# A recommender tower on one core: the first group's products by selection matmuls, layer 0 in three-matmul form, and work moved between GpSimd, ScalarE and VectorE

## The reference

```python
# e: (512, 32 fields, 32);  filter_0: (32*32, 128);  filter_1: (32*128, 128)
z   = einsum('bhd,bmd->bhmd', e, e).reshape(b, 32*32, d)
c   = relu(einsum('bpd,pn->bnd', z, filter_0))
z1  = einsum('bhd,bmd->bhmd', e, c).reshape(b, 32*128, d)
c1  = relu(einsum('bpd,pn->bnd', z1, filter_1))
h   = concat([c.sum(-1), c1.sum(-1), dense_ctx], axis=1)
y   = relu(relu(h @ W_top1 + b_top1) @ W_top2 + b_top2) @ W_top3
```

## Time and profile before

| | us |
|---|---|
| median of 3 runs | 870.16 (868.09 to 870.87) |
| profiled execution, whole | 867.69 |
| its span, first to last instruction | 865.9 |
| TensorE busy, share of the span | 842.2 (97%) |
| ScalarE | 798.3 (92%) |
| GpSimd | 754.7 (87%) |
| VectorE | 747.8 (86%) |

### The profile page before, as it was taken

The page is one execution under the profiler, slowest core; times in us unless marked ns, Lnnn a source line. Parts: engine busy times, 40 slices in busy tenths (PEclk is TensorE's granted clock), DMA queues, the critical chain, the costliest instruction groups (busy, mean ns, idle before and its releaser), DMA issues.

```text
span 865.9 us, 16597 instructions
## 1 busy us (share of the span) xinstructions
PE 842.2 (97%) x3584; PEld 667.0 (77%) x3584; DVE 747.8 (86%) x800; ACT 798.3 (92%) x2781; POOL 754.7 (87%) x544
## 2 busy tenths in 40 slices
PE   2899999999999999999999999999999999999998
PEld 1688777778877777887777887777788777788776
DVE  4588888998888898888889888889888888988894
ACT  2699999999999999999999999999999999999994
POOL 5599999999999999999999999999999899997661
PEclk9999999999999999999999999999999999999999
DMA  5452222212222211222221222222122222122000
GB/s 163 140 148 83 77 81 83 60 34 78 80 77 81 80 47 44 82 76 80 82 79 28 64 82 76 80 81 54 36 81 79 77 81 69 35 69 73 2 1 1
DMA packets 42924, 61.11 MB, mean 71 GB/s; under 512 B 6259, under 2 KB 17139, under 8 KB 42902
## 3 DMA queue, kind: packets, MB, share of 16 engines
q1 hardware_dynamic: 38806, 58.75, 22.2%
q0 software_dynamic: 4096, 2.11, 1.6%
HBM read 56.64 MB, written 4.20 MB: 70 GB/s over the span
## 4 chain that ended last, share of the span: by engine, by line
PE 94%; DVE 2%; DMA 2%; issue 1%; SPq 0%; POOL 0%; ACT 0%; DVEq 0%; POOLq 0%
PE ps_y L685 27%; PE ps_y L686 27%; PE ps_y L691 27%; PE ps_c L664 6%; PE ps_c L674 2%; PE ps_c L672 2%; PE ps_c L673 2%; DVE csum L581 1%; PE ps_c L670 1%; DMA second<-et_scratch 1%; DVE prod L568 1%; DMA gat<-table,rows_now 1%; PE ps_h L696 0%; POOL gat L306 0%; DMA et_scratch<-gat 0%
## 5 line engine op out<-in xcount | busy, mean ns | idle before, releaser
L433 ACT ACTIVATE prod<-ps_y,es 128x128 f32<-128x128 f32 x2560 | 720.8, 456 | 26.8 <-PE ps_y L691 21.0
L581 DVE TENSOR_REDUCE csum<-prod 128x64 f32<-128x1536 f32 x256 | 446.4, 1744 | 0.1
L685 PE MATMUL ps_y<-w_hi,c_hi 128*128 128x512 f32 x1024 | 428.5, 419 | 0.9 <-ACT c_hi L394 0.5
L691 PE MATMUL ps_y<-w_hi,c_lo 128*128 128x512 f32 x1024 | 400.2, 391 | 0.0
L686 PE MATMUL ps_y<-w_lo,c_hi 128*128 128x512 f32 x1024 | 400.1, 391 | 0.0
L568 DVE TENSOR_TENSOR prod<-ps_y,es 128x512 f32<-128x512 f32 x384 | 259.0, 681 | 89.9 <-PE ps_y L691 89.8
L344 POOL TENSOR_TENSOR prod<-prod 128x1024 f32<-128x1024 f32 x128 | 309.1, 2415 | 27.4 <-ACT prod L433 22.0
L685 PEld LDWEIGHTS ps_y<-w_hi,c_hi 128*128 128x128 f32 x1024 | 192.5, 188 | 56.3 <-issue 10.5
L686 PEld LDWEIGHTS ps_y<-w_lo,c_hi 128*128 128x128 f32 x1024 | 192.5, 188 | 53.7 <-issue 14.9
L691 PEld LDWEIGHTS ps_y<-w_hi,c_lo 128*128 128x128 f32 x1024 | 192.2, 188 | 42.1
L335 POOL TENSOR_TENSOR z<-first,second 128x512 f32<-128x512 f32 x155 | 198.7, 1304 | 9.7 <-DMA second<-et_scratch 9.7
(11 more groups left out here) (96 smaller groups left out, 287.2 us busy)
## 6 DMA issues: line engine op xcount, KB each, us to landing
second<-et_scratch SPq DMA_DIRECT2D x160, 256.0 KB, 4.3
first<-et_scratch SPq DMA_DIRECT2D x32, 256.0 KB, 3.3
et_scratch<-gat SPq DMA_DIRECT2D x64, 64.0 KB
prod<-w SPq DMA_DIRECT2D x4, 512.0 KB, 7.8
gat<-table,rows_now POOLq DMA_INDIRECT x128, 2.4
wt_sb<-wt SPq DMA_DIRECT2D x2, 512.0 KB
prod<-w0a SPq DMA_DIRECT2D x1, 320.0 KB, 3.3
prod<-w0b SPq DMA_DIRECT2D x1, 320.0 KB, 3.3
```

Of the source, the lines that this page charges most:

```text
L433: last = nc.scalar.activation(prod[:, buffer_of(g, u), h // 2, :, h % 2], ps_y[:, bank_of(g, u, k), j * N:(j + 1) * N], ACT.Copy, scale=es ...
L581: nc.vector.tensor_reduce(csum[:, g.r, maps, u], prod[:, buffer_of(g, u), FOLD // 2:F // 2, maps, :].rearrange("p a n t -> p n a t"), AX.X ...
L685: nc.tensor.matmul(out, hi, w_hi, start=True, stop=False)
L691: nc.tensor.matmul(out, lo, w_hi, start=False, stop=True).then_inc(y_ready, 1)
```

## The change

1. **Head.** Group 0 no longer goes through the HBM scratch. A table `picks` of zeros and ones is loaded (its place zeroed first by POOL), and PE multiplies the gathered rows by it: 6 loads of 4 fp32 matmuls with 128 columns put `first` and the five `second` into PSUM banks. ACT copies `first` out, DVE multiplies (chunk 4 first). Chunks 0 to 3 of group 0 stay fp32. `filter_1`'s first quarter is loaded ahead of `filter_0`, the others after the first gather; its rounding is spread over the head and group 0. The warm-up is 10 matmuls and no longer waits for the gather. The first three groups' gathers read their indices without a staging copy.
2. **Layer 0** from group 1 on: `WHOLE = 0`, so chunks 0 and 1 are split too: two more `z_hi` on ACT, two more `z_lo` on POOL, three fp32r matmuls each in place of one fp32 matmul.
3. **`h0`** is summed by DVE from `c_hi` and `c_lo` side by side (1024 columns in place of 512), and ACT's `rectify_whole` goes.
4. **Parts** are rectified by POOL, behind its fold of `u = 1`.
5. **Fold.** `FOLD = 6`: POOL adds 3 field pairs to 3 (768 columns in place of 1024), DVE sums 13 pairs in place of 12.
6. **Staging** of the indices is a DMA that SP issues one group early.

The diff, cut to its core:

```diff
-WHOLE = 2
+WHOLE = 0
-WARM_UP = 22
+WARM_UP = 10
+FIRST_ROWS = SLOTS * TG
+PICKS = {"first": 0, 0: 1, 1: 2, 2: 3, 3: 4, 4: 5}
+PICK_ORDER = (4, 0, 1, 2, 3)
-FOLD = F // 4
+FOLD = 6
...
+        picks_sb = sb("picks_sb", [P, BT, 2, P + P // 2])
+        c_both = sb("c_both", [P, SLOTS, 2 * COLS], F32R)
...
             sp.dma_start(bounds_sb[:, :], bounds).then_inc(ids_in, 16)
+            filters(0)
             sp.dma_start(w0a_sb, w0a).then_inc(w0_in, 16)
             sp.dma_start(w0b_sb, w0b).then_inc(w0_in, 16)
             sp.dma_start(copy_sb[:, :], copy_of).then_inc(w0_in, 16)
+            sp.wait_ge(picks_zeroed, 1)
+            for q in range(BT):
+                sp.dma_start(picks_sb[q * F:(q + 1) * F, q, :, :], picks).then_inc(picks_in, 16)
             sp.dma_start(ones_b[:, :], ones_of_b).then_inc(ones_in, 16)
+            sp.wait_ge(gathered[0], 16 * TG)
+            for n in range(1, W1_LOADS):
+                filters(n)
+            def stage(g):
+                sp.dma_start(rows_now[:, g.r, :], rows[:, bass.ds(g.times(TG), TG)]).then_inc(rows_staged, 16)
+            def pairs(g, following=False):
                 cols = g.times(COLS)
                 sp.wait_ge(gathered[g.r], g.uses(16 * TG))
                 sp.sem_inc(sp_passed, 1)
+                if following:
+                    stage(g.plus(1))
...
-            pairs(Group(0, 0))
             for g in range(1, SLOTS):
                 pairs(Group(0, g))
...
                 if 0 in tiles:
-                    stage(g)
+                    pool.wait_ge(es_ready, g.times(1, 1 - SLOTS))
+                    wait(pool, et_written, g.times(32, -32 * SLOTS))
+                    pool.wait_ge(rows_staged, g.times(16, 16 * (1 - SLOTS)))
+                    pool.sem_inc(pool_passed, 1)
...
+            def rectify_parts(g):
+                pool.wait_ge(reduced, g.times(TG * HALVES, TG * HALVES))
+                wait(pool, c1_ready, g.times(1))
+                pool.sem_inc(pool_passed, 1)
+                nc.gpsimd.tensor_scalar(c1_parts[:, :, :], csum[:, g.r, :, :], 0.0, None, ALU.max).then_inc(parts_rectified, 1)
...
+            nc.gpsimd.memset(picks_sb[:, :, :, :], 0.0).then_inc(picks_zeroed, 1)
             pool.wait_ge(rows_step, 5)
-            for g in range(SLOTS):
-                gather(Group(0, g), range(TG))
+            for n in range(FIRST_ROWS):
+                pool.indirect_dma_start(
+                    out=gat[:, n // TG, n % TG * D:(n % TG + 1) * D], out_offset=None, in_=table,
+                    in_offset=bass.IndirectOffsetOnAxis(ap=rows[:, n:n + 1], axis=0),
+                ).then_inc(gathered[n // TG], 16)
-            Z_AT = {0: ((1, 1), (1, 2), (1, 3)), 1: ((1, 4),), 3: ((2, 0),)}
-            Z_LO_AT = {1: (2, 3), 2: (4,)}
+            Z_AT_FIRST = {0: ((1, 0), (1, 1), (1, 2)), 1: ((1, 3), (1, 4)), 3: ((2, 0), (2, 1))}
+            Z_LO_AT_FIRST = {1: (0, 1), 2: (2, 3, 4)}
+            Z_AT = {0: ((1, 2), (1, 3)), 1: ((1, 4),), 3: ((2, 0), (2, 1))}
+            Z_LO_AT = {0: (0, 1), 1: (2, 3), 2: (4,)}
...
                     fold(g, u)
+                    if u == 1 and number != 0:
+                        rectify_parts(g.plus(-1))
...
+            round_w1((0, 1))
+            act.wait_ge(picked, 1)
+            nc.scalar.activation(first[:, :], ps_y[:, PICKS["first"], :], ACT.Copy).then_inc(first_copied, 1)
+            act.wait_ge(w0_in, 48)
+            act.wait_ge(z_ready, 1)
+            nc.scalar.activation(z_hi[:, LASTK, :], z[:, LASTK, :], ACT.Copy, scale=copy_sb[:, 0:1]).then_inc(z_hi_ready, SPLIT)
+            round_w1((2, 3, 4, 5))
+            rectify_first(slice(0, 1), first_c_hi)
+            rectify_first(slice(1, TG), c_hi_ready)
+            round_w1((6, 7))
...
-                        if (u, k) == (1, 6) and number != 0:
-                            rectify_parts(g.plus(-1))
-                        if more and (u, k) == (3, 6):
-                            rectify_whole(g.plus(1))
-            Z_HI_AT = {(1, 2): (0, 4), (1, 3): (0, 6), (1, 4): (1, 5)}
+            Z_HI_AT = {(2, 0): (3, 4), (2, 1): (3, 7), (1, 2): (0, 2), (1, 3): (0, 5), (1, 4): (1, 5)}
...
+            def multiply_picked(k, place):
+                dve.wait_ge(picked, place)
+                nc.vector.tensor_tensor(z[:, k, :], first[:, :], ps_y[:, PICKS[k], :], ALU.mult).then_inc(z_ready, 1)
...
-                dve.wait_ge(c_ready, g.times(1, 1))
+                dve.wait_ge(c_lo_ready, g.times(1, 1))
                 nc.vector.tensor_reduce(
-                    h0[:, bass.ds(g.times(GB), GB)], c[:, :].rearrange("p (o b d) -> p b o d", b=GB, d=DT),
+                    h0[:, bass.ds(g.times(GB), GB)],
+                    c_both[:, g.r, :].bitcast(F32).rearrange("p (o b d) -> p b o d", b=GB, d=DT),
                     AX.XY, ALU.add).then_inc(h0_done, 1)
...
+            rest_w1(0)
+            rest_w1(1)
+            dve.wait_ge(first_copied, 1)
+            for place, k in enumerate(PICK_ORDER):
+                multiply_picked(k, place + 2)
+                if place in (2, 3):
+                    rest_w1(place)
...
-            pe.wait_ge(es_ready, 1)
             for n in range(WARM_UP):
                 nc.tensor.matmul(ps_y[:, 0, :], w0_hi[:, 0, :], w0_hi[:, 0:BANK // N, :].rearrange("p k n -> p (k n)"),
                                  start=True, stop=True)
+            pe.wait_ge(picks_in, 16 * BT)
+            pe.wait_ge(gathered[0], 16 * TG)
+            for load in ("first",) + PICK_ORDER:
+                table_of, shift = {"first": (1, 0), LASTK: (1, P // 2)}.get(load) or (0, 16 * load)
+                for q in range(BT):
+                    last = nc.tensor.matmul(ps_y[:, PICKS[load], q * P:(q + 1) * P], picks_sb[:, q, table_of, shift:shift + P],
+                                            gat[:, 0, :], start=True, stop=True)
+                last.then_inc(picked, 1)
...
-            Z_USED_AT = ((0, 6), (1, 2), (1, 6), (2, 2), (2, 6))
+            Z_USED_AT_FIRST = ((1, 3), (1, 6), (2, 2), (2, 5), (2, 7))
+            Z_USED_AT = ((1, 1), (1, 4), (2, 1), (2, 4), (2, 6))
```

More of the change, by code:

```diff
@@ L291, in body @@
                 if number is None or number + SLOTS < GROUPS:
-                    pairs(g.plus(SLOTS))
+                    pairs(g.plus(SLOTS), number is None or number + SLOTS + 1 < GROUPS)
             over_groups(sp, body)
@@ L436, in scale, with round_w1 @@
                 last.then_inc(act_scaled, 1)
[L438 to L448, removed]
+            def round_w1(banks):
+                for k in banks:
+                    act.wait_ge(w1_in[k * W1_LOADS // NK], 16)
+                    nc.scalar.activation(w1_hi[:, k * HB:(k + 1) * HB, :], w1_raw[:, k * HB:(k + 1) * HB, :],
+                                         ACT.Copy).then_inc(w1_hi_ready, 1)
+            round_w1((0, 1))
[8 more added lines that the diff above has]
+            round_w1((6, 7))
             def body(g, number):
@@ L453, in body @@
                     for k in range(NK):
+                        if number == 0 and (u, k) == (2, 0):
+                            act.wait_ge(w1_lo_ready, NK)
                         if k in ACT_BANKS[u]:
@@ L657, in _, with layer0 @@
         def _(pe):
-            def layer0(g, k):
+            def layer0(g, k, number=None):
                 if k == 0:
-                    wait(pe, c_ready, g.times(1))
-                if k < WHOLE:
-                    pe.wait_ge(z_ready, g.times(KP, k + 1))
+                    wait(pe, c_lo_ready, g.times(1))
+                if k < WHOLE or (number == 0 and k < LASTK):
+                    if number == 0:
+                        pe.wait_ge(z_ready, PICK_ORDER.index(k) + 1)
+                    else:
+                        pe.wait_ge(z_ready, g.times(KP, k + 1))
                     nc.tensor.matmul(ps_c[:, :], w0_sum[:, k, :], z[:, k, :].rearrange("p (b o d) -> p o b d", b=GB, d=DT),
@@ L681, in layer1 @@
                     wait(pe, dve_scaled, signals(DVE_BANKS, g, u, k - RING))
+                if number == 0 and u == 0:
+                    pe.wait_ge(w1_lo_ready, k + 1)
                 out = ps_y[:, bank_of(g, u, k), :]
@@ L684, in layer1 @@
                 w_hi, w_lo = (x[:, k * HB:(k + 1) * HB, :].rearrange("p h n -> p (h n)") for x in (w1_hi, w1_lo))
-                nc.tensor.matmul(out, hi, w_hi, start=True, stop=False)
-                nc.tensor.matmul(out, hi, w_lo, start=False, stop=False)
+                if "hi" in parts:
+                    nc.tensor.matmul(out, hi, w_hi, start=True, stop=False)
+                    nc.tensor.matmul(out, hi, w_lo, start=False, stop=False)
+                if "lo" not in parts:
+                    return
                 if number == 0 and u == 0 and k == 0:
@@ L805, in filters_by_bank, with row_picks @@
     return out.reshape(N, F, N)
+def row_picks():
+    step, same = (np.zeros((F, P + P // 2), np.float32) for _ in range(2))
+    for p in range(P + P // 2):
+        step[(p // SH + p % SH) % F, p] = 1
```

(2 more changed lines are left out.)

144 lines of the change are left out of this document (69 added, 75 removed).

## The result

The changed kernel takes 894.96 us (median of 6 runs, 893.43 to 895.29) against 869.85 (6 runs) before: a ratio of 1.0297 [1.0284, 1.0311]. The forecast was 864.3 with a range of 857 to 880, so both the sign and the range were missed. The profiled execution took 894.12 us, its span is 892.1: 26.2 more than before, and 32.1 more than the prediction's sum of 860.0. The times and ratios in this document leave out two of the ten executions of `copy_parts`, which took 1406 and 1706 us.

A forecast was written before the change was run, and what follows sets the result against it. It took TensorE (25.50 us a group) as the bound, replaced by GpSimd at 25.43. Group 0, 28 GpSimd groups, three TensorE groups and the tail sum to 860.0, 5.9 under the span; 870.16 - 5.9 = 864.3 us, range 857 to 880.

The forecast's parts named there:

- the last term of the GpSimd paragraph: GpSimd's rectify of the parts, put at 0.72 us a group on top of 24.71, giving 25.43.
- first sign of being wrong: In GpSimd's steady group: the prediction would be wrong above all if the rectify costs 1 us or more.
- The rival on the other side: GpSimd's rectify costs 1.25 us like its other 512-column operations; group 25.96, median 879, slower; chance 0.18.
- R: Time of GpSimd's rectify in each group: 0.72 us forecast, break-even 0.93, slower by over 0.3% above 1.03.
- the prediction's estimate from that page: GpSimd's rectify at line rate: 0.43 plus a fixed 0.13, 0.56 us; the sum would then be 859.8.
- Its cost is nothing: SP issues one more DMA per group, ahead of the scratch writes, hidden by a scratch transfer read a group later.
- Third, the head: Before layer 1: warm-up from 10.4, layer 1 at 25.6 us in place of 30.69, GpSimd's first product for group 1 at 27.0.
- TensorE's loss at (1, 3): In group 0, TensorE waits for GpSimd at its first use of group 1's work, losing 1.4 us.
- Fourth, the tail: Behind layer 1's end: 19.6 us plus 0.7 for five longer VectorE sums, 20.3 us.
- its 24.71 us without the rectify: GpSimd's steady group: products, rests, folds and gathers, before the rectify is added.
- TensorE's 0.33 a group: Steady group: splitting two fp32 chunks into three fp32r matmuls each saves 0.33 us, leaving TensorE 25.17.
- a VectorE bound: Rival: VectorE, with 24.41 us of work, sets a group of 25.76 us; median 876; chance 0.09.

The follow-up runs named there:

- copy_parts: The changed kernel with GpSimd copying the parts in place of rectifying them (the maximum left out); 870.60 to 873.37 us in eight executions, ratio 1.0036.
- early_stage: The changed kernel with SP's first staging DMA (group 3's indices) sent ahead of the first pair loads; 891.3 us against 868.69, ratio 1.0254.
- late_only: The changed kernel with group 1's five chunks used later in group 0's TensorE program; 892.42 us against 869.96, ratio 1.0257.
- act_rect: The changed kernel with the parts rectified by ScalarE again, at (1, 6), as before; 864.66 us against 868.69, ratio 0.9952.
- act_whole2: The changed kernel with ScalarE rectifying and chunks 0 and 1 as fp32 matmuls again in all groups; 876.37 us against 869.96, ratio 1.0077.
- act_early_late_warm: The changed kernel with ScalarE rectifying, first staging DMA early, group 1's chunks used later, eight extra matmuls in the tail; 861.12 us against 869.96, ratio 0.9893.
- best: ScalarE rectifying, early first staging, group 1's chunks later, eight tail matmuls, and the fold of 8 fields in the last group; 861.68 us against 868.69.

## Why the prediction was wrong

**The step that failed first** is the last term of the GpSimd paragraph: "From below it costs the copy of four numbers, 0.19; from above the two-input operation of the same shape, 1.25. I take the middle, 0.72". Neither end was a bound: an instruction with one tile and a number takes 1.47 us, more than one with two tiles. The prediction's own first sign of being wrong, a rectify of 1 us or more, is the one that came. The error of 0.75 us counts 28 times: 21 us of the 32 by which the sum missed. The rival on the other side had the right mechanism (R decides from 0.93) and a price that was too low, 1.25, so that its 879 and the upper end, 880, were too low as well; with 1.47 in its place it gives 0.22 x 28 = 6 us more, 885. What the Trainium skill's GPSIMD Engine Reference, § 4.1 (Engine selection), says of one-input work at line rate holds here for a copy (0.62 us, 0.56 by the prediction's estimate from that page) and not for an instruction with a number in it (1.50).

**Second, "Its cost is nothing" (SP).** In steady groups that is right: the first gather's gap is 0.16. Once, in group 0, the DMA stands in SP's queue behind two groups' pair loads and GpSimd waits 3.47 us. I looked at what it hides behind in the loop and not at its first issue; `early_stage` shows its price of 3.3 us.

**Third, the head.** The warm-up's start was 1.5 us too early (`w_sum` at 9.38 where I had 8.0), and the order of VectorE's program was not followed: two rests of 0.6 stand between the products. So GpSimd's first product comes at 30.13, not 27.0; the 4.7 us between VectorE's last product and it was right (5.0). Those 3.1 us and the 3.5 of the staging are 6.6 on GpSimd's program; it leaves group 0 at 60.9, where the prediction had 54.4. TensorE's loss at (1, 3) was 3.0, not 1.4, and the clock at 0.50 behind it was not foreseen at all; while GpSimd sets the pace that costs little more (0.9 us at the last mark in `late_only`), but with ScalarE's rectify it and the staging together hold `act_rect` 2.0 us back.

**Fourth, the tail.** I had added 0.7 to 19.6; it is 24.0. VectorE's sums account for 1.7, and 2.4 is the dense matmuls, half of which went every 0.43 us at a granted clock of 0.50.

The terms close: 21 + 0.8 (28 steps of 26.21 and not 26.18) + 6.6 + 3.7 (24.0 and not 20.3) = 32.1.

**What was right:** which engine becomes the bound, and its 24.71 us without the rectify; TensorE's 0.33 a group (0.34 in `act_whole2`, and 25.18 in `act_rect`); VectorE's halves (1.878 us) and ScalarE below TensorE; the fold at 1.81; the picks (6.12 us, 6.7 forecast). Of the rivals, a VectorE bound is excluded by the step of 25.18.

What stays open: why the tail's clock falls in `act_early_late_warm` and not in `best`, though TensorE is given the same work there, and why the first product of the head comes at 20.32, some 2 us behind the pass that it seems to need.

## What to carry to other kernels

Where a term is multiplied by the number of groups and no row of the trace has that form of instruction, "between the nearest rows" is not a bound: measure it, or take the dearest row and ask whether the change survives it (here 1.25: still too low, but enough to show a loss). When work is taken off one engine and given to one with a quarter of a microsecond to spare, add up the new engine's group before anything else. And when two waits cover each other, repairing either alone shows nothing; repair both before judging.

## What the hardware showed that was not expected

- On GpSimd, 128 x 512 fp32: a copy 0.62 us, two tiles 1.25 to 1.30, one tile with a number (maximum or product) 1.49 to 1.50.
- After a stop of 3.0 us in group 0 TensorE's granted clock read 0.50, and matmuls of 512 columns went every 0.43 us in place of 0.23 for 6 us, though TensorE was then busy all the time; in the tail it read 0.50 again behind a stop of 2.0 us and a row of small matmuls, and 12 of the 24 dense ones went at the slower pace.
- A DMA of 2 KB, issued on SP right behind six pair loads of 256 KB, landed 5.4 us after its issue; the median of its 30 issues is 1.7.
